# Turning the feed-forward inputs by DMA and VectorE in place of TensorE, in a one-core block of attention and ternary feed-forward

## What is computed

```python
x = x + _layernorm(attention(_layernorm(x)))          # 16 heads of 128, causal, rotary, decayed keys and values
gu = _layernorm(x) @ ternary(w_gate_up).T             # 256 -> 2 * 1024
gate, up = split(gu)
h = silu(gate) * up
z = rms_norm(h) @ ternary(w_proj).T                   # 1024 -> 256
x = x + _layernorm(z)
```

## Time and profile before

| what | value |
|---|---|
| median of three runs | 1040.01 us (1039.96 to 1041.44) |
| the profiled execution | 1039.91 us |
| its span in the profile | 1038.1 us |
| mean granted TensorE clock | 0.997 |
| instructions | 25078 |
| busy PE, DVE, ACT, POOL | 98%, 80%, 84%, 90% of the span |

### The profile page before, as it was taken

How to read it: one execution, slowest core, us unless ns; L and a number is a source line. 1 busy time by engine, 2 the same in 40 slices (tenths; PEclk the granted TensorE clock), 3 DMA queues, 4 the chain that set the end, 5 groups by cost and what they waited for, 6 DMA issues and landing times.

```text
span 1038.1 us, 25078 instructions
## 1 busy us (share of the span) xinstructions
PE 1021.4 (98%) x7827; PEld 981.6 (95%) x7827; DVE 827.1 (80%) x2841; ACT 868.2 (84%) x2399; POOL 931.4 (90%) x926
## 2 busy tenths in 40 slices
PE   7999999999999999999999999999999999999996
PEld 6899999999999999999999999999999999999996
DVE  6868888878887888788888888887777767677776
ACT  5988898989898989898989898889898867877774
POOL 4899999999999999999999999999999847877775
PEclk9999999999999999999999999999999999999998
DMA  7561121112112110121122112111131000000001
GB/s 262 187 184 43 42 63 41 43 52 68 44 36 61 63 42 33 62 63 42 33 68 67 42 39 75 43 42 53 42 113 31 2 1 11 22 24 29 22 22 41
DMA packets 35124, 58.56 MB, mean 56 GB/s; under 512 B 3136, under 2 KB 16000, under 8 KB 34688
## 3 DMA queue, kind: packets, MB, share of 16 engines
q1 hardware_dynamic: 34992, 56.96, 17.2%
HBM read 50.92 MB, written 9.18 MB: 58 GB/s over the span
## 4 chain that ended last, share of the span: by engine, by line
POOL 60%; PE 19%; issue 14%; DVE 1%; POOLq 0%; ACT 0%; ACTq 0%; DVEq 0%
POOL arena L599 15%; POOL arena L622 14%; POOL arena L633 13%; POOL arena L609 13%; PE psum L1017 12%; PE psum L1057 6%; POOL arena L581 1%; POOL arena L557 1%; POOL X L590 1%; PE psum L775 1%; PE psum L1030 1%; POOL arena L565 0%; PE psum L1039 0%; POOLq L303 0%; POOL arena L572 0%
## 5 line engine op out<-in xcount | busy, mean ns | idle before, releaser
L633 POOL TENSOR_TENSOR arena<-arena 128x768 f32<-128x768 f32 x128 | 196.2, 1533 | 8.9 <-DVE arena L1580 8.3
L609 POOL TENSOR_TENSOR arena<-arena 128x512 f32<-128x512 f32 x128 | 174.0, 1359 | 10.0
L1593 DVE SCALAR_TENSOR_TENSOR pt_split<-psum,vh_col,pt_split 128x256 fp32r<-128x256 f32 (+1 forms) x512 | 177.0, 407 | 3.5 <-ACT pt_split L1252 3.0
L599 POOL TENSOR_TENSOR arena<-arena,tables 128x512 f32<-128x512 f32 x128 | 166.9, 1304 | 13.7 <-ACT arena L1222 13.0
L622 POOL TENSOR_TENSOR arena<-arena 128x512 f32<-128x512 f32 x127 | 162.9, 1283 | 0.0
L929 PE MATMUL psum<-arena 128*128 128x256 f32 x512 | 153.9, 382 | 3.1 <-POOL arena L609 1.8
L775 PE MATMUL psum<-wo_hi,o_hi 128*128 128x256 f32 x512 | 152.1, 297 | 0.0
L1233 ACT ACTIVATE arena<-arena 128x256 f32<-128x256 f32 x256 | 128.6, 502 | 26.7 <-DVE arena L1570 20.1
L775 PE MATMUL psum<-xt_lo,wq_hi 128*128 128x256 f32 x512 | 144.7, 283 | 0.0
L775 PE MATMUL psum<-xt_hi,wq_lo 128*128 128x256 f32 x512 | 144.5, 282 | 0.0
L775 PE MATMUL psum<-wo_hi,o_lo 128*128 128x256 f32 x512 | 144.3, 282 | 0.0
(11 more groups left out here) (195 smaller groups left out, 3405.7 us busy)
## 6 DMA issues: line engine op xcount, KB each, us to landing
arena<-kh_rows SPq DMA_DIRECT2D x127, 256.0 KB, 3.3
out<-spare SPq DMA_DIRECT2D x15, 256.0 KB, 2.1
arena<-w_rows SPq DMA_DIRECT2D x6, 512.0 KB, 4.8
X<-L_attn_Wout SPq DMA_DIRECT2D x1, 2048.0 KB, 14.5
X<-L_attn_x SPq DMA_DIRECT2D x1, 2048.0 KB, 12.5
arena<-L_attn_Wq SPq DMA_DIRECT2D x1, 1536.0 KB, 10.0
X<-L_attn_x SPq DMA_DIRECT2D x1, 1536.0 KB, 9.7
w_rows<-L_ffn_w_gate_up SPq DMA_DIRECT2D x3, 512.0 KB, 8.2
```

The source lines that it names most:

```text
L599: nc.gpsimd.tensor_tensor(swap, swap, spread, ALU.mult).then_inc(q_sined, 1)
L609: nc.gpsimd.tensor_tensor(q_rot[p % 2], q_cos[p % 2], q_swap[p % 2], ALU.add).then_inc(q_roped, 1)
L633: nc.gpsimd.tensor_tensor(tb, tb, r.unsqueeze(3).to_broadcast([P, HP, 3, P]), ALU.mult).then_inc(p_ready, 1)
L1593: last = nc.vector.scalar_tensor_tensor(pt_lo[p % 2][:, o], b[:, i], vh[:, t, h:h + 1], pt_hi[p % 2][:, o].bitcast(F32), ALU.mult, ALU.sub ...
```

## The change

For units 1 to 15 the input is turned in two moves. A 128 by 128 turn is a turn of 32 by 32 blocks each, which VectorE's transpose does inside 32 partitions, and a placing of the blocks across partitions, which transfers do.

- ScalarE's `norm_x2` writes its rows in another order of 32-element runs (`by_rows`), so that one transfer's 128 columns lie together.
- SP issues four transfers a unit (`spread_blocks`) from the normalised rows to the new buffer `moved`, each from 128 partitions of 128 elements to 32 partitions of 512, once `norm_x2` is done and the transpose before has read the buffer. The stores are unrolled, with the moves of unit u + 4 behind the store of unit u.
- VectorE's new `turn_x2` transposes all 32 by 32 blocks of `moved` in one instruction into `F_BANK`. It stands behind `fold_squares` and ahead of `stats_x2`.
- TensorE's `turn_x2` is only called for unit 0.
- ScalarE's `norm_x2` moves up, from behind `activate` 1 to ahead of `high_hidden` 0.

```diff
+        moved = sb("moved", [P, NT * E])
...
+        by_rows = lambda rows, t: rows.rearrange("p t e -> p (t e)").rearrange("p (b k t c) -> p t k b c", b=4, k=ET, t=NT)[:, t]
+        by_blocks = lambda x_tile: x_tile.rearrange("p (k b c) -> p k b c", k=ET, b=4)
+        moved_in = moved[:, :].rearrange("p (a g c) -> p g a c", a=4, c=P // 4)
+        turned_out = F_BANK.rearrange("p (g q a) -> p a g q", a=4, q=P // 4)
...
+            def spread_blocks(rows, landed):
+
+                flat = rows.rearrange("p t e -> p (t e)")
+                for b in range(4):
+                    sp.dma_start(moved[b * 32:(b + 1) * 32, :].rearrange("q (a g) -> q a g", a=4),
+                                 flat[:, b * P:(b + 1) * P]).then_inc(landed, 16)
...
-            with sp.Fori(0, BATCH - 3, 2) as u:
-                for i in range(2):
-                    rows = out_rows[:, bass.ds(address((u + i) * NT), NT), :]
-                    sp.wait_ge(res_done, u + i + 1)
-                    sp.dma_start(rows, res[i]).then_inc(stored[i], 16)
+
+            def move_x2(u):
+
+                sp.wait_ge(x2_norm, u * NT + NT)
+                sp.wait_ge(x2_turned, u)
+                spread_blocks(x2_rows(u, u % 2), x2_moved)
+
+            for u in range(1, 4):
+                move_x2(u)
+            for u in range(BATCH - 2):
+                sp.wait_ge(res_done, u + 1)
+                sp.dma_start(out_rows[:, u * NT:(u + 1) * NT, :], res[u % 2]).then_inc(stored[u % 2], 16)
+                if u + 4 < BATCH:
+                    move_x2(u + 4)
...
                 at = unit_at(u0, s, FLAG["turn"])
-                if at and at[0] > 0:
-                    turn_x2(*at)
...
-                    nc.scalar.activation(x2_rows(u, i)[:, t, :], x_batch(u)[:, t, :], ACT.Identity, bias=x2_bias[:, t:t + 1],
+                    o, i_ = x2_rows(u, i)[:, t, :], x_batch(u)[:, t, :]
+                    if u > 0:
+                        o, i_ = by_rows(x2_rows(u, i), t), by_blocks(i_)
+                    nc.scalar.activation(o, i_, ACT.Identity, bias=x2_bias[:, t:t + 1],
                                          scale=x2_rstd[:, t:t + 1]).then_inc(x2_norm, 1)
...
-                if at:
-                    if at[0] > 0:
-                        activate(*at, 0)
-                    high_hidden(*at, 0)
-                    activate(*at, 1)
+                if at and at[0] > 0:
+                    activate(*at, 0)
                 at = unit_at(u0, s, FLAG["norm"])
                 if at and at[0] > 0:
                     norm_x2(*at)
+                at = unit_at(u0, s, FLAG["up"])
+                if at:
+                    high_hidden(*at, 0)
+                    activate(*at, 1)
...
+            def turn_x2(u):
+
+                dve.wait_ge(x2_moved, u * 64)
+                dve.wait_ge(x2_lo_done, u)
+                nc.vector.transpose(turned_out, moved_in).then_inc(x2_turned, 1)
+
...
+                at = unit_at(u0, s, FLAG["turn"])
+                if at and at[0] > 0:
+                    turn_x2(at[0])
                 at = unit_at(u0, s, FLAG["stats"])
                 if at and at[0] > 0:
                     stats_x2(at[0])
```

More of the change, by code:

```diff
@@ L242, in sandwich_kernel @@
         heads = lambda ap, n: ap.rearrange("p (h n) -> p h n", n=n)
+        by_rows = lambda rows, t: rows.rearrange("p t e -> p (t e)").rearrange("p (b k t c) -> p t k b c", b=4, k=ET, t=NT)[:, t]
+        by_blocks = lambda x_tile: x_tile.rearrange("p (k b c) -> p k b c", k=ET, b=4)
+        moved_in = moved[:, :].rearrange("p (a g c) -> p g a c", a=4, c=P // 4)
+        turned_out = F_BANK.rearrange("p (g q a) -> p g a q", a=4, q=P // 4)
         consts = sem("consts")
@@ L284, in sandwich_kernel @@
         wgu_placed, wpr_placed = sem("wgu_placed"), sem("wpr_placed")
+        x2_moved = sem("x2_moved")
         x2_stats, x2_aggr, x2_eps, x2_neg, x2_inv, x2_biased, x2_norm, x2_turned, x2_hi_done, x2_lo_done = (
```

## The result

The changed kernel takes 1049.56 us in the median of six runs (1048.85 to 1052.36), against 1040.05 for the kernel before; the ratio is 1.0097, interval 1.0082 to 1.0111. It is slower by 9.5 us, as forecast in sign, four times the 2.4 us of the sum, and 0.06 us above the range's end of 1049.5. One correction to the code under "The change": in the kernel `turned_out` is `F_BANK.rearrange("p (g q a) -> p g a q", ...)`.

The account below looks back on a forecast made before the run. TensorE, busy 98%, bounds the kernel, with VectorE's row 0.44 us behind; 13 periods × 0.21 − 0.44 (unit 15) + 0.1 (unit 1) = +2.4 us on 1039.91 gives 1042.3, range 1040.3 to 1049.5.

Parts of the forecast that it names:

- VectorE's row decides: VectorE between down products and split_x2: anything added there moves the next unit's start once 0.44 us are spent.
- The gain of 0.44: TensorE: dropping the 4 turning products saves 0.44 us a unit.
- the slack: Between the end of VectorE's split_x2 and TensorE's next unit: 0.44 us, all spent by shortening TensorE's side.
- a step of 0.65: VectorE's transpose of 128×512 f32: ordinary operation's 0.60 us plus 0.04 to fill a block, together 0.65.
- The rival of half rate: VectorE's transpose takes two passes, step 1.20 us: +9.5 us, so 1049.4; chance 0.10.
- the one of double rate: VectorE's transpose passes two elements at a time, step 0.30 us: −2.2 us, so 1037.8; win's chance 0.05.
- the transfers' landing: SP's four moves: landed 2.96 us after the normalisation, 1.1 us ahead of the transpose.
- the 4.06 that were there: From norm_x2's end to the transpose wanting its rows: 4.50 us, less 0.44 for ScalarE's later round.
- The slow bound: SP's four moves at their slowest: 0.05 + 3 × 0.50 + 3.3 = 4.85 us, 0.79 too late.
- The clock: TensorE, idle about 0.65 us in each 12.4, gets a lower granted clock; chance 1 in 50.
- Unit 1: The first unit with moved rows, no down products yet: the turn's gain is lost, taken as +0.1 us.
- Late transfers: VectorE stands waiting before the transpose: 1053.4 at the slow bound, 1045 for 0.2 us of lateness; chance 0.17.

Follow-up runs that it names:

- the doubled transpose: Against the kernel without transfers (1043.63 us), a second transpose that waits for the first: 1053.63 us.
- the statistics first: Changed kernel with stats_x2 moved ahead of stats_z in VectorE's order: 1039.50 us with transfers, 1035.63 without.
- the kernel with the moves ahead of the store: Changed kernel with norm_x2 of units 2 to 15 moved 3.3 us earlier and SP's moves issued ahead of the output store: 1047.08 us.

## Why the prediction was off

- **VectorE's row decides.** Right, and shown by the doubled transpose and by the statistics first. The gain of 0.44 held (11.73 against 12.17), and the slack came out within 0.05 us: 0.63 − 0.44 = +0.19 a period by the sum, +0.16 where the fold was undisturbed.
- **The transpose.** Taken as a step of 0.65, measured 0.63 (0.71 to 0.73 recorded). The rival of half rate is out, and so is the one of double rate. The Trainium skill (Vector Engine (DVE) Microarchitecture Reference, section 3.8) says that the transposing array sustains one element per cycle per lane; the trace agrees, with 0.72 us for 512 elements against 0.69 for an ordinary operation. The estimate of 0.76 from the Trainium skill (VectorE: DVE Perf Modes, The three transpose paths) was 0.04 high.
- **The sum for the row.** Forecast +0.21 a period, measured 12.48 − 12.17 = +0.31; where the fold was undisturbed, 12.33, it was +0.16. The fold's 0.16 beside GpSimd comes on top, a term I didn't have, though the kernel before had a fold of 1.21 in its trace. Unit 15 gave its 0.44 back (11.73). The whole row cost 3.1 us by the medians, against 2.4.
- **The failed step: the transfers' landing.** The prediction says: "For 64 KB between SBUF rows I take 1.8: 1.16 + 1.8 = 2.96, so 1.1 us are left." The issues stand 0.64 apart and not 0.37, so the last leaves at 1.9 to 2.0, and lands after 2.2: 4.1 and not 2.96, and nothing is left of the 4.06 that were there. The spacing of 0.37 was the larger error: it came from two other kinds of issue. The slow bound in the text, 4.85, was nearer than the value taken, and the spread was not priced at all: with the median at the edge, every slow issue (up to 3.95 for four) and landing (up to 3.7) costs at least its full excess. In units 2 to 15 VectorE waited 4.3 us for rows in the profiled execution.
- **The clock.** Given 1 chance in 50, and priced by the stretches of 0.65 us in which TensorE would be idle; after those it did stay at 1.00. It fell once in the profiled execution, behind an idle stretch of 2.36 us that late rows made, and cost 1.5 us. So the price of late transfers in the sum, one us for one us, was too low. The other executions have no trace here; the mean granted clock of all six is 0.995 to 0.997, against 0.997 to 0.999 without transfers.
- **Unit 1.** Forecast +0.1. The head shows −0.43 without transfers and +1.2 with them, so the turn's gain was there and the late rows cost 1.6 in the profiled execution.
- **The rivals.** Late transfers (0.17) named the cause; the time that it gives lay between my two figures, 1045 for 0.2 us of lateness and 1053.4 for the bound. The range left out "the upper part" of this case. The sum was right in sign for the reason that it gives, 3.1 of the 9.5 us; that the range nearly held the measured time is owed to the two rivals that widened it.
- **Nothing else.** SP's store ahead of the moves cost nothing in the changed kernel (it ends when the rows are ready), and the order of ScalarE cost nothing.

The split of the 9.5 us is then 3.1 for the row, measured with the transfers left out, and the rest, 5.9 to 6.4, for the transfers. That rest is a difference, not a second measurement. In the traces, of which the changed kernel's is 2.8 us above its median, the two kernels differ by 7.9 us behind the table load: 1.6 at unit 1, 4.3 of waits in later units, 1.5 of the clock, and 0.5 that is not assigned.

## What to carry to other kernels

Work taken off the busiest engine is worth what the next chain has to spare: find the anchor that both share (here the end of the down products), and count what is placed behind it. The same change with the following statistics placed ahead of the anchor instead won 0.1% with late transfers and 0.3 to 0.4% once they were on time. For a short transfer in several pieces, price the issues by rows of the same kind of issue and not by the quickest pair, and when the slow bound comes out late, take the spread as a cost; also look at which wait stands ahead of the issue in its queue.

## What the runs showed that was not expected

- An issue of a 64 KB copy from SBUF to SBUF with 512 bytes a run kept SP for 0.60 us in the median (0.55 to 2.07), 0.64 from one to the next, against 0.38 for the 256 KB store beside it. The landing took 2.1 to 3.7 us, median 2.2, and one copy of 256 KB was in time where four of 64 KB weren't.
- The slowest issues are not scattered. In all four kernels with SP's order as changed and four moves a unit, the fourth move of unit 9 held SP 1.25 to 2.07 us, the first of unit 4 0.73 to 1.22 and the first of unit 13 0.92 to 1.45. With the moves ahead of the store they fall in other units. No run shows why.
- TensorE's granted clock fell to the 1.2 GHz level for 3.4 us behind an idle stretch of 2.36 us in the changed kernel, and for as long behind one of 2.81 in the kernel with the moves ahead of the store.
- VectorE's 256-element addition of SBUF operands took 0.39 alone; when it began beside a GpSimd operation with more than 0.11 us to run it ended 0.28 us behind that operation's end, so that it took 0.54 to 0.57 in most periods and up to 1.46. One of 512 elements took 1.73 in place of 0.69 beside GpSimd, before and after.
